# Two layers of cross attention on one core: the product with Wv and the next q taken in turn on TensorE

## The chip, the cores and the metric

The kernel runs on one core of one Trainium2 chip. The metric is the time of the whole program on the device in microseconds (us); lower is better. The kernel before has a median of 1026.28 us over three runs (1025.25 to 1026.63).

## What is computed

There are 32 batch entries, `x` of 224 rows by 512 and a context of 750 rows by 256. Two layers of the same form run one after the other on x; the context is the same for both:

```
q = x Wq + bq ;  k = ctx Wk + bk ;  v = ctx Wv + bv
w = softmax over t of (q k^T / sqrt(512))      # over the 224 rows of x, for each context row
x = layernorm(w v + x) * gamma + beta          # eps 1e-6
```

The softmax runs over the rows of x, so each context row can be normalised by itself. All is in float32.

## The kernel before, in words

**Algebra.** Scores need q k^T only, so the kernel folds `Wq Wk^T` once per layer into a matrix `A` (512 by 256) and multiplies x by it: what it calls q is `x A`, transposed, 256 by 224, held as two halves `l` = 0, 1 of 128 partitions. In the same way w is first multiplied by the raw context (the `o` product, again two halves `l`) and the result by `Wv` (the `pv` product, two halves `h` of 112 rows each). The operands of q, score and pv are split into a rounded high part and a low remainder of type float32r; each product is then high times high, high times low and low times high.

**Units.** A unit is one layer of one batch entry. `a` units are layer 0, `b` units layer 1; a b unit works on the entry whose layer 0 was done three units before. For each unit TensorE makes, in this order: q (two products of 12 matmuls with 224 moving columns and 128 columns of weights), the scores (three pairs of context pieces, 12 matmuls each), o (two products of six float32 matmuls, which the profile records as 12 each), and pv (two products of six matmuls, 512 moving columns, 112 columns of weights). In steady state one pass of the loop body (`turn`) does one a unit and one b unit; each engine has its own `turn`, an order written out by hand, and the engines meet through semaphores only. Each engine takes its instructions in that order, and a wait holds up all that stands behind it on the same engine.

**TensorE's order around the change** (lines 765 to 788). At two places of a pass pv and q products stand next to each other. At the b place the order is pv(b-1,0), q(b,0), pv(b-1,1), q(b,1), and then o(a,0); pv(b-1) belongs to the b unit of the pass before. At the a place it is q(a+1,0), pv(a,0), spread_d(a+1) (two small transposes), pv(a,1), q(a+1,1), and then o(b,0).

**Who takes the results.** ScalarE's `turn` (lines 933 to 967): when a q half is complete (`q_ready`) `q_hi` (L882) rounds it into `qT_hi`; `exps` (L890) makes the exponentials of three context pieces; `normalise` (L906) multiplies three pieces by the inverse sums and raises `probs_done`, after which TensorE may use these pieces in an o product: the first three matmuls of `o_product(u, 0)` need the first three pieces, the other three the second. ScalarE's order around the a place is `q_hi(a+1,0)`, `normalise(b,0)`, `exps(b,1)`, `normalise(b,1)`, `q_hi(a+1,1)`. Around the b place it is `exps(a,0)`, `xT_hi(b,1)`, `xT_hi(a+1,0)`, `exps(a,1)`, `q_hi(b,0)`, `normalise(a,0)`, `normalise(a,1)`, `q_hi(b,1)`. Both layers share the code; the names are as the turn that runs on TensorE has them.

VectorE's `turn` (lines 1271 to 1336) makes the low remainders (`q_lo` L1148, `o_lo` L1187, `xT_lo_part` L1117), adds pv to the residual (`add_pv` L1220), and inverts the exponential sums (`invert_sum` L1181). Around the a place its order has `residual(a,0)`, `residual(a,1)`, `score_max(b,3)`, `invert_sum(b,0)`, `o_lo(a,1)`, two `score_max`, `ctxT_lo`, `add_pv(a,0)`, `q_lo(a+1,0)`, `turn_ctx`, `invert_sum(b,1)`, `half_moments(a,0)`, `add_pv(a,1)` and, some instructions later, `q_lo(a+1,1)`.

**What the products wait for.** `q_product(u, l)` waits until the PSUM bank it shares with o has been read (`oT_lo_done` of the unit two before, and `resid_done` for l = 1), and for the parts of xT. `pv_product(u, h)` waits until its bank was read by the unit before (`y_done`), and for `oT_hi` and `oT_lo`.

Of the kernel before, what the change touches and what calls it, by code (L numbers as in the profile page):

```python
# [14 lines left out]
R_HALF = 1  # L15
# [72 lines left out]
def build_xattn(nc, x, ctx, weights, out):  # L88
    B, T, E = x.shape
    _, M, L = ctx.shape  # L90
    P = 128
    TP, TH = T // 2, 2
    MC = 6
    MP = M // MC
    EC, LC = E // P, L // P
# [9 lines left out]
    with ExitStack() as stack:  # L105
        def sb(name, shape, dt=F32):
            return stack.enter_context(nc.sbuf_tensor(name, shape, dt))

        def bank(name):
            return stack.enter_context(nc.psum_tensor(name, [P, 512], F32))  # L110

        def sem(name):
            return stack.enter_context(nc.semaphore(name))


        A_hi = sb("A_hi", [P, LAYERS, EC, L], F32R)
        A_lo = sb("A_lo", [P, LAYERS, EC, L], F32R)
        Wv_hi = sb("Wv_hi", [P, LAYERS, LC, E], F32R)
        Wv_lo = sb("Wv_lo", [P, LAYERS, LC, E], F32R)
# [29 lines left out]
        xT_hi = sb("xT_hi", [P, 2, EC, T], F32R)  # L149
        xT_lo = sb("xT_lo", [P, 2, EC, T], F32R)  # L150
# [11 lines left out]
        oT_hi = sb("oT_hi", [P, LC, T], F32R)  # L162
        oT_lo = sb("oT_lo", [P, LC, T], F32R)
# [19 lines left out]
        oq_bank = [bank("oq_bank0"), bank("oq_bank1")]  # L183
        pv_bank = [bank("pv_bank0"), bank("pv_bank1")]
# [16 lines left out]
        bq_done = sem("bq_done")  # L201
        A_ready = sem("A_ready")
        A_hi_done = sem("A_hi_done")
        A_lo_done = sem("A_lo_done")
# [5 lines left out]
        Wv_lo_done = sem("Wv_lo_done")  # L210
# [10 lines left out]
        ctxT_lo_done = sem("ctxT_lo_done")  # L221
        xT_ready = sem("xT_ready")
        xT_hi_done = sem("xT_hi_done")
        xT_lo_done = sem("xT_lo_done")
# [3 lines left out]
        q_ready = sem("q_ready")  # L228
# [11 lines left out]
        oT_hi_done = sem("oT_hi_done")  # L240
        oT_lo_done = sem("oT_lo_done")
        resid_done = sem("resid_done")
        pv_ready = sem("pv_ready")
        y_done = sem("y_done")
# [32 lines left out]
        def units(i, j):  # L277

            return (lambda d: Unit(2 * (i + d), j)), (lambda d: Unit(2 * (i + d) + 1, j))
# [14 lines left out]
        PIECES_OF_PAIR = [-(-2 * (p + 1) * MP // PC) for p in range(HALF)]  # L294
# [9 lines left out]
        def is_last(u):  # L304

            return u.j is None and u.u == LAST
# [150 lines left out]
        def _(pe):  # L457
# [110 lines left out]
            def spread_d(u):  # L568

                if not u.real:  # L570
                    return
                pe.wait_ge(dot_done, u.n(m=2))
                b = t_bank[0]
                if u.layer:

                    pe.wait_ge(xT_lo_done, u.n(m=2))
                elif u.past(-1):

                    pe.wait_ge(d_done, u.n(-1))
                else:  # L580

                    pe.wait_ge(ctxT_lo_done, PIECES)
                for h in range(TH):
                    ins = nc.tensor.transpose(b[:, h * TP:(h + 1) * TP], d_col[0:TP, h:h + 1].to_broadcast([TP, P]),
                                              ident[0:TP, 0:TP])
                ins.then_inc(d_ready, 1)

            def q_product(u, l):
                if not u.real:
                    return  # L590
                if u.first and l == 0:
                    pe.wait_ge(A_lo_done, EC * (u.layer + 1))
                if u.first and u.layer == 0:

                    pe.wait_ge(ctxT_lo_done, PIECES_OF_PAIR[l])
                if u.past(-2):

                    pe.wait_ge(oT_lo_done, u.n(-2, 2, l - 1))
                    if l == R_HALF:
                        pe.wait_ge(resid_done, u.n(-2, 2))  # L600
                o = oq_bank[l][:, 0:T]
                for e in range(EC):
                    if l == 0 and e % 2 == 0:
                        pe.wait_ge(xT_hi_done, u.n(m=2, add=e // 2 - 1))
                    nc.tensor.matmul(o, A_hi[:, u.layer, e, l * P:(l + 1) * P], xT_hi[:, u.par, e, :], start=(e == 0), stop=False)  # L605
                    nc.tensor.matmul(o, A_lo[:, u.layer, e, l * P:(l + 1) * P], xT_hi[:, u.par, e, :], start=False, stop=False)  # L606
                for e in range(EC):
                    if l == 0 and e % 2 == 0:
                        pe.wait_ge(xT_lo_done, u.n(m=2, add=e // 2 - 1))
                    ins = nc.tensor.matmul(o, A_hi[:, u.layer, e, l * P:(l + 1) * P], xT_lo[:, u.par, e, :],  # L610
                                           start=False, stop=(e == EC - 1))
                ins.then_inc(q_ready, 1)

            def score_product(u, p):
                if not u.real:
                    return
                if u.layer == 0:
                    pe.wait_ge(ctxT_hi_done, u.batch(PIECES, PIECES_OF_PAIR[p]))
                    pe.wait_ge(ctxT_lo_done, u.batch(PIECES, PIECES_OF_PAIR[p]))
                if u.past(-1) or p == 2:  # L620

                    pe.wait_ge(smax_done, u.n(m=6, add=2 * p - 8))
                b = score_bank[(u.pair0() + p) % 2]
                for c in range(2):
                    cols = slice((2 * p + c) * MP, (2 * p + c + 1) * MP)
                    o = b[0:MP, c * T:(c + 1) * T]
                    for l in range(LC):
                        if p == 0 and c == 0:
                            pe.wait_ge(qT_hi_done, u.n(m=2, add=l - 1))
                        nc.tensor.matmul(o, cT_hi[:, u.slot, l, cols], qT_hi[:, l, :], start=(l == 0), stop=False)  # L630
                        nc.tensor.matmul(o, cT_lo[:, u.slot, l, cols], qT_hi[:, l, :], start=False, stop=False)  # L631
                    for l in range(LC):
                        if p == 0 and c == 0:
                            pe.wait_ge(qT_lo_done, u.n(m=2, add=l - 1))
                        ins = nc.tensor.matmul(o, cT_hi[:, u.slot, l, cols], qT_lo[:, l, :], start=False, stop=(l == LC - 1))  # L635
                ins.then_inc(s_ready, 1)

            def o_product(u, l):
# [22 lines left out]
                                               start=True, stop=True)  # L661
                ins.then_inc(o_ready, 1)

            def pv_product(u, h, at_end=False):
                if not u.real or is_last(u) != at_end:
                    return
                if u.past(-1):

                    pe.wait_ge(y_done, u.n(-1, 2, h - 1))
                if u.first and h == 0:  # L670
                    pe.wait_ge(Wv_lo_done, u.layer + 1)
                if u.first and u.layer == 0:

                    pe.wait_ge(bq_done, h + 1)
                o = pv_bank[h][0:TP, :]
                rows = slice(h * TP, (h + 1) * TP)
                for l in range(LC):
                    if h == 0:
                        pe.wait_ge(oT_hi_done, u.n(m=2, add=l - 1))
                    nc.tensor.matmul(o, oT_hi[:, l, rows], Wv_hi[:, u.layer, l, :], start=(l == 0), stop=False)  # L680
                    nc.tensor.matmul(o, oT_hi[:, l, rows], Wv_lo[:, u.layer, l, :], start=False, stop=False)  # L681
                for l in range(LC):
                    if h == 0:
                        pe.wait_ge(oT_lo_done, u.n(m=2, add=l - 1))
                    ins = nc.tensor.matmul(o, oT_lo[:, l, rows], Wv_hi[:, u.layer, l, :], start=False, stop=(l == LC - 1))
                ins.then_inc(pv_ready, 1)

            def last_o_product(u):

# [75 lines left out]
            def turn(i, j):  # L765
                a, b = units(i, j)
                score_product(a(+0), 0)
                o_product(b(-1), 1)
                transpose_x(b(+0), 0)
                score_product(a(+0), 1)  # L770
                score_product(a(+0), 2)
                transpose_x(b(+0), 1)
                pv_product(b(-1), 0)
                q_product(b(+0), 0)
                pv_product(b(-1), 1)
                q_product(b(+0), 1)
                o_product(a(+0), 0)
                spread_d(b(+0))
                score_product(b(+0), 0)
                score_product(b(+0), 1)  # L780
                o_product(a(+0), 1)
                score_product(b(+0), 2)
                q_product(a(+1), 0)
                pv_product(a(+0), 0)
                spread_d(a(+1))
                pv_product(a(+0), 1)
                q_product(a(+1), 1)
                o_product(b(+0), 0)
            turns(pe, turn, 2)
            last_o_product(last_unit)  # L790
# [813 lines left out]
```

## Time and profile before

| | us |
|---|---|
| median of three runs | 1026.28 |
| time of the profiled execution | 1024.44 |
| its span, first to last instruction | 1022.3 |
| TensorE matmul busy | 992.1 (97%) |
| VectorE busy | 874.6 (86%) |
| ScalarE busy | 664.2 (65%) |
| GpSimd busy | 566.7 (55%) |

The profile is of one execution; the span leaves out 2.1 us around it. Busy time of TensorE counts each matmul from its start to its modelled end, and consecutive matmuls overlap, so 97% says that TensorE hardly ever stood empty, not that it ran at its peak. The cadence has to be read from the starts of consecutive matmuls. A row "x4" of the timeline merges four like instructions; its duration runs from the first start to the last end.

### The profile page before, as it was taken

The numbers are of one execution on the slowest core, as the hardware profiler recorded it, in microseconds if no ns is written. First come the engines' busy times: TensorE is split into PE (matmuls) and PEld (weight loads), VectorE is DVE, ScalarE is ACT, GpSimd is POOL, SyncE is SP. The second block draws the span as 40 slices with busy tenths as digits, with TensorE's granted clock in tenths as the row PEclk, the third lists the DMA queues.
The fourth block names the chain that finished last, engine by engine and source line by source line (L and its number), as shares of the span: only waits on it lengthen the run. The fifth ranks groups of instructions, "written<-read, shape, count | busy, mean of one in ns | idle before, by whom it ended". The sixth has DMA issues, their size and how long they took to land. (4 is left out here: it accounts for less than half of the span.)

```text
span 1022.3 us, 23872 instructions
## 1 busy us (share of the span) xinstructions
PE 992.1 (97%) x6948; PEld 932.4 (91%) x6948; DVE 874.6 (86%) x2609; ACT 664.2 (65%) x1864; POOL 566.7 (55%) x520
## 2 busy tenths in 40 slices
PE   6889999999999999999999999999999999999986
PEld 5789999999999999999999999999999999999975
DVE  3768889898889889888988988898988898888867
ACT  2456667667666767766666776766676677667642
POOL 0114655565665556566555656555565655556574
PEclk9979999999999999999999999999999999999998
DMA  8643345444444544444554443455444345544101
GB/s 229 134 96 74 79 98 115 97 98 101 95 83 100 114 96 96 99 89 87 104 114 96 95 99 82 91 106 110 95 96 100 79 94 110 103 105 98 54 19 37
DMA packets 374246, 98.84 MB, mean 97 GB/s; under 512 B 308520, under 2 KB 357818, under 8 KB 374202
## 3 DMA queue, kind: packets, MB, share of 16 engines
q1 hardware_dynamic: 371370, 96.98, 43.7%
q10 hardware_dynamic: 2832, 1.32, 0.6%
q8 instruction: 22, 0.36, 0.1%
q14 instruction: 22, 0.18, 0.1%
HBM read 83.59 MB, written 14.68 MB: 96 GB/s over the span
## 5 line engine op out<-in xcount | busy, mean ns | idle before, releaser
L654 PE MATMUL oq_bank<-probs,raw 125*128 125x224 f32 x1512 | 307.5, 353 | 3.7 <-ACT probs L906 3.7
L654 PEld LDWEIGHTS oq_bank<-probs,raw 125*128 125x128 f32 x1512 | 276.7, 190 | 4.5 <-issue 3.2
L890 ACT ACTIVATE probs<-probs,neg_max 125x224 f32<-125x224 f32 x378 | 177.8, 472 | 143.5 <-DVE neg_max L1165 143.5
L1477 POOL TENSOR_TENSOR psum<-probs 125x672 f32<-125x672 f32 x63 | 101.6, 1613 | 285.0 <-ACT probs L906 285.0
L630 PE MATMUL score_bank<-qT_hi,cT_hi 128*125 128x224 f32 x768 | 199.8, 287 | 2.8 <-ACT cT_hi L847 1.7
L631 PE MATMUL score_bank<-qT_hi,cT_lo 128*125 128x224 f32 x768 | 189.1, 273 | 0.0
L906 ACT ACTIVATE probs<-probs,rsum 125x224 f32<-125x224 f32 x378 | 150.7, 471 | 10.3 <-DVE rsum L1181 8.9
L1540 POOL TENSOR_TENSOR y_out<-z,gamma_row 112x512 f32<-112x512 f32 x62 | 93.8, 1534 | 114.7 <-ACT z L930 114.7
L630 PEld LDWEIGHTS score_bank<-qT_hi,cT_hi 128*125 128x125 f32 x768 | 145.3, 189 | 7.8 <-issue 5.5
L635 PE MATMUL score_bank<-qT_lo,cT_hi 128*125 128x224 f32 x768 | 147.2, 273 | 0.0
L631 PEld LDWEIGHTS score_bank<-qT_hi,cT_lo 128*125 128x125 f32 x768 | 145.5, 189 | 0.0
L1165 DVE CUSTOM_DVE_ANT_0 probs<-score_bank,d_row 125x224 f32<-125x224 f32 x384 | 139.0, 380 | 6.7 <-PE score_bank L635 3.8
L605 PE MATMUL oq_bank<-xT_hi,A_hi 128*128 128x224 f32 x512 | 121.7, 276 | 0.9 <-DVE w_col L1057 0.6
L606 PE MATMUL oq_bank<-xT_hi,A_lo 128*128 128x224 f32 x512 | 121.5, 275 | 0.0
L1210 DVE SCALAR_TENSOR_TENSOR y<-bv_row,oq_bank,x 112x512 f32<-112x512 f32 x126 | 105.5, 857 | 18.4 <-ACT oT_hi L917 18.3
L635 PEld LDWEIGHTS score_bank<-qT_lo,cT_hi 128*125 128x125 f32 x768 | 115.1, 189 | 0.2 <-DVE qT_lo L1148 0.2
L680 PE MATMUL pv_bank<-Wv_hi,oT_hi 128*112 128x512 f32 x256 | 105.2, 411 | 0.0
L1117 DVE TENSOR_TENSOR xT_lo<-t_bank,xT_hi 128x448 fp32r<-128x448 f32 x128 | 78.8, 616 | 30.2 <-ACT xT_hi L862 30.1
L605 PEld LDWEIGHTS oq_bank<-xT_hi,A_hi 128*128 128x128 f32 x512 | 98.4, 192 | 6.7 <-DVE w_col L1057 0.8
L606 PEld LDWEIGHTS oq_bank<-xT_hi,A_lo 128*128 128x128 f32 x512 | 98.6, 193 | 3.8
L930 ACT ACTIVATE z<-y,nmr,rstd 112x512 f32<-112x512 f32 x126 | 95.5, 806 | 9.7 <-DVE nmr L1252 9.7
L681 PE MATMUL pv_bank<-Wv_lo,oT_hi 128*112 128x512 f32 x256 | 100.6, 393 | 0.0
(122 smaller groups left out, 2024.7 us busy)
## 6 DMA issues: line engine op xcount, KB each, us to landing
raw<-in_ctx_dram SPq DMA_DIRECT2D x64, 375.0 KB
cb<-in_ctx_dram SPq DMA_DIRECT2D x248, 92.0 KB
x<-in_x_dram SPq DMA_DIRECT2D x32, 448.0 KB, 3.6
xb<-in_x_dram SPq DMA_DIRECT2D x124, 112.0 KB, 3.0
out_dram<-y_out SPq DMA_DIRECT2D x31, 448.0 KB, 6.6
cb<-in_ctx_dram SPq DMA_DIRECT2D x124, 3.5 KB
y<-in_L_xattn_Wq_dram SPq DMA_DIRECT2D x2, 512.0 KB, 5.4
Wq_next<-in_L_xattn_Wq_dram SPq DMA_DIRECT2D x2, 512.0 KB, 15.7
```

What stands on the lines that cost most here:

```text
L605: nc.tensor.matmul(o, A_hi[:, u.layer, e, l * P:(l + 1) * P], xT_hi[:, u.par, e, :], start=(e == 0), stop=False)
L606: nc.tensor.matmul(o, A_lo[:, u.layer, e, l * P:(l + 1) * P], xT_hi[:, u.par, e, :], start=False, stop=False)
L630: nc.tensor.matmul(o, cT_hi[:, u.slot, l, cols], qT_hi[:, l, :], start=(l == 0), stop=False)
L631: nc.tensor.matmul(o, cT_lo[:, u.slot, l, cols], qT_hi[:, l, :], start=False, stop=False)
L635: ins = nc.tensor.matmul(o, cT_hi[:, u.slot, l, cols], qT_lo[:, l, :], start=False, stop=(l == LC - 1))
L654: ins = nc.tensor.matmul(o, raw[0:MP, u.slot, c, cols], probs[0:MP, u.par4, c, :], start=(c == 0), stop=(c == MC - 1))
L680: nc.tensor.matmul(o, oT_hi[:, l, rows], Wv_hi[:, u.layer, l, :], start=(l == 0), stop=False)
L890: ins = act.activation(probs[0:MP, u.par4, c, :], probs[0:MP, u.par4, c, :], ACT.Exp, bias=neg_max[0:MP, u.par4, c:c + 1], scale=-1.0, acc ...
L906: ins = act.activation(probs[0:MP, u.par4, c, :], probs[0:MP, u.par4, c, :], ACT.Identity, scale=rsum[0:MP, u.par4, c:c + 1])
L1165: dve.tensor_tensor_reduce(probs[0:MP, u.par4, c, :], b[0:MP, (c % 2) * T:(c % 2 + 1) * T], d_row[0:MP, :], -SCALE, 3.4e38, ALU.add, ALU.m ...
L1210: dve.scalar_tensor_tensor(out=y[0:TP, u.par, h, :], in0=bv_row[0:TP, u.layer, :], scalar=(last_r if at_end else r_psum)[:, h:h + 1], in1= ...
L1477: pool.tensor_tensor(psum3[0:MP, :, :], probs[0:MP, u.par4, 0:HALF, :], probs[0:MP, u.par4, HALF:MC, :], ALU.add).then_inc(psum3_done, 1)
```

## The change

`q_product` and `pv_product` are cut into single matmuls, `q_step` and `pv_step`, with the same waits ahead of the same matmuls. A new function issues one pv matmul and then two q matmuls, six times over. The turn calls it at both places. No matmul, wait or transfer is added or removed; the other engines' programs are untouched. Where one of the two units doesn't exist, or the pv is that of the last unit, the two products are issued whole, pv first. The opening, which is written out by hand, keeps whole products.

```diff
+            Q_STEPS, PV_STEPS = 3 * EC, 3 * LC
+            def q_step(u, l, k):
+                if k == 0:
+                    ... the waits of q_product
+                if k < 2 * EC:
+                    e = k // 2
+                    if l == 0 and k % 4 == 0:
+                        pe.wait_ge(xT_hi_done, u.n(m=2, add=e // 2 - 1))
+                    of = A_lo if k % 2 else A_hi
+                    nc.tensor.matmul(o, of[:, u.layer, e, cols], xT_hi[:, u.par, e, :], start=(k == 0), stop=False)
+                    return
+                e = k - 2 * EC
+                if l == 0 and e % 2 == 0:
+                    pe.wait_ge(xT_lo_done, u.n(m=2, add=e // 2 - 1))
+                ins = nc.tensor.matmul(o, A_hi[:, u.layer, e, cols], xT_lo[:, u.par, e, :], start=False, stop=(e == EC - 1))
+                if e == EC - 1:
+                    ins.then_inc(q_ready, 1)
+            def pv_step(u, h, k):
+                ... in the same way, one of the six matmuls of pv_product
+            def pv_with_q(u, h, v, l):
+                if not (u.real and v.real) or is_last(u):
+                    pv_product(u, h)
+                    q_product(v, l)
+                    return
+                for k in range(PV_STEPS):
+                    pv_step(u, h, k)
+                    q_step(v, l, 2 * k)
+                    q_step(v, l, 2 * k + 1)
 def turn(i, j):
-                pv_product(b(-1), 0)
-                q_product(b(+0), 0)
-                pv_product(b(-1), 1)
-                q_product(b(+0), 1)
+                pv_with_q(b(-1), 0, b(+0), 0)
+                pv_with_q(b(-1), 1, b(+0), 1)
                 ...
                 score_product(b(+0), 2)
-                q_product(a(+1), 0)
-                pv_product(a(+0), 0)
+                pv_with_q(a(+0), 0, a(+1), 0)
                 spread_d(a(+1))
-                pv_product(a(+0), 1)
-                q_product(a(+1), 1)
+                pv_with_q(a(+0), 1, a(+1), 1)
                 o_product(b(+0), 0)
```

## Rows read from the trace of the kernel before

**Rows 1.** The page: busy time by engine; TensorE's granted clock in tenths, 40 slices.

```profile
PE 992.1 (97%) x6948; PEld 932.4 (91%) x6948; DVE 874.6 (86%) x2609; ACT 664.2 (65%) x1864; POOL 566.7 (55%) x520
PEclk9979999999999999999999999999999999999998
```

**Rows 2.** Windows, steady state: stretch, length, busy (count) by engine, clock, DMA.

```profile
110.00:953.00 843.00, 842.47 (x5976) 796.05 (x5975) 747.58 (x2255) 580.66 (x1634) 498.28 (x449) 1.00 0.45 97
```

**Rows 3.** Waits of TensorE, matmuls then weight loads: total us, times, longest.

```profile
PE oq_bank L654 <- ACT probs L906: 3.7, 3, 2.0
...
PEld pv_bank L685 <- DVE oT_lo L1187: 4.7, 13, 1.0
```

**Rows 4.** Timeline of TensorE, the a place: start, us, instruction, count.

```profile
503.04 0.27 PE L605 MATMUL oq_bank<-xT_hi,A_hi 128*128 128x224 f32 x1
...
533.10 0.27 PE L605 MATMUL oq_bank<-xT_hi,A_hi 128*128 128x224 f32 x1
...
533.99 0.61 PE L610 MATMUL oq_bank<-xT_lo,A_hi 128*128 128x224 f32 x4
534.44 0.40 PE L680 MATMUL pv_bank<-Wv_hi,oT_hi 128*112 128x512 f32 x1
...
535.83 0.36 PE L584 MATMUL t_bank<-ident,d_col 112*128 112x112 f32 x2
535.95 0.47 PE L680 MATMUL pv_bank<-Wv_hi,oT_hi 128*112 128x512 f32 x1
...
536.95 0.62 PE L685 MATMUL pv_bank<-Wv_hi,oT_lo 128*112 128x512 f32 x2
537.41 0.27 PE L605 MATMUL oq_bank<-xT_hi,A_hi 128*128 128x224 f32 x1
...
538.74 2.44 PE L654 MATMUL oq_bank<-probs,raw 125*128 125x224 f32 x12
...
562.88 0.27 PE L605 MATMUL oq_bank<-xT_hi,A_hi 128*128 128x224 f32 x1
```

**Rows 5.** Timeline of ScalarE, same place; in brackets the idle time ahead and its releaser.

```profile
534.72 0.45 ACT L882 ACTIVATE qT_hi<-oq_bank,c_col 128x224 fp32r<-128x224 f32 x1 [0.69 <-PE oq_bank L610]
535.07 1.21 ACT L906 ACTIVATE probs<-probs,rsum 125x224 f32<-125x224 f32 x3
536.18 0.47 ACT L890 ACTIVATE probs<-probs,neg_max 125x224 f32<-125x224 f32 x1
...
537.92 1.23 ACT L906 ACTIVATE probs<-probs,rsum 125x224 f32<-125x224 f32 x3 [0.24 <-DVE rsum L1181]
```

**Rows 6.** Timeline near the end: an o product that waited for ScalarE.

```profile
984.32 1.30 PE L654 MATMUL oq_bank<-probs,raw 125*128 125x224 f32 x6
986.46 0.83 PE L654 MATMUL oq_bank<-probs,raw 125*128 125x224 f32 x3 [0.84 <-ACT probs L906]
...
985.18 1.23 ACT L906 ACTIVATE probs<-probs,rsum 125x224 f32<-125x224 f32 x3 [0.24 <-DVE rsum L1181]
```

**Rows 7.** Timelines of TensorE, ScalarE, VectorE at the b place.

```profile
518.51 0.47 PE L680 MATMUL pv_bank<-Wv_hi,oT_hi 128*112 128x512 f32 x1
518.82 0.39 PE L681 MATMUL pv_bank<-Wv_lo,oT_hi 128*112 128x512 f32 x1
...
519.09 0.95 ACT L862 ACTIVATE xT_hi<-t_bank 128x448 fp32r<-128x448 f32 x2
...
521.78 0.69 DVE L1220 TENSOR_TENSOR y<-pv_bank,y 112x512 f32<-112x512 f32 x1
```

**Rows 8.** Timelines of VectorE and TensorE: the other kind of pass, a place.

```profile
505.14 0.35 DVE L1187 TENSOR_TENSOR oT_lo<-oq_bank,oT_hi 128x224 fp32r<-128x224 f32 x1
...
505.31 0.73 PE L685 MATMUL pv_bank<-Wv_hi,oT_lo 128*112 128x512 f32 x2
```

**Rows 9.** Timeline of VectorE after the a place.

```profile
537.71 0.18 DVE L1181 RECIPROCAL rsum<-ssum 125x3 f32<-125x3 f32 x1
...
540.51 0.44 DVE L1148 SCALAR_TENSOR_TENSOR qT_lo<-oq_bank,c_col,qT_hi 128x224 fp32r<-128x224 f32 x1
```

More of the change, by code:

```diff
@@ L586, in spread_d @@
                 ins.then_inc(d_ready, 1)
+            Q_STEPS, PV_STEPS = 3 * EC, 3 * LC
+            def q_step(u, l, k):
+                if k == 0:
+                    if u.first and l == 0:
+                        pe.wait_ge(A_lo_done, EC * (u.layer + 1))
+                    if u.first and u.layer == 0:
+                        pe.wait_ge(ctxT_lo_done, PIECES_OF_PAIR[l])
+                    if u.past(-2):
+                        pe.wait_ge(oT_lo_done, u.n(-2, 2, l - 1))
+                        if l == R_HALF:
+                            pe.wait_ge(resid_done, u.n(-2, 2))
+                o = oq_bank[l][:, 0:T]
+                cols = slice(l * P, (l + 1) * P)
+                if k < 2 * EC:
[11 more added lines that the diff above has]
+                    ins.then_inc(q_ready, 1)
             def q_product(u, l):
@@ L590, in q_product @@
                     return
[L591 to L612, printed above, removed]
+                for k in range(Q_STEPS):
+                    q_step(u, l, k)
             def score_product(u, p):
@@ L662, in o_product @@
                 ins.then_inc(o_ready, 1)
+            def pv_step(u, h, k):
+                if k == 0:
+                    if u.past(-1):
+                        pe.wait_ge(y_done, u.n(-1, 2, h - 1))
+                    if u.first and h == 0:
+                        pe.wait_ge(Wv_lo_done, u.layer + 1)
+                    if u.first and u.layer == 0:
+                        pe.wait_ge(bq_done, h + 1)
+                o = pv_bank[h][0:TP, :]
+                rows = slice(h * TP, (h + 1) * TP)
+                if k < 2 * LC:
+                    l = k // 2
+                    if h == 0 and k % 2 == 0:
+                        pe.wait_ge(oT_hi_done, u.n(m=2, add=l - 1))
+                    of = Wv_lo if k % 2 else Wv_hi
+                    nc.tensor.matmul(o, oT_hi[:, l, rows], of[:, u.layer, l, :], start=(k == 0), stop=False)
+                    return
+                l = k - 2 * LC
+                if h == 0:
+                    pe.wait_ge(oT_lo_done, u.n(m=2, add=l - 1))
+                ins = nc.tensor.matmul(o, oT_lo[:, l, rows], Wv_hi[:, u.layer, l, :], start=False, stop=(l == LC - 1))
+                if l == LC - 1:
+                    ins.then_inc(pv_ready, 1)
             def pv_product(u, h, at_end=False):
@@ L666, in pv_product @@
                     return
[L667 to L686, printed above, removed]
+                for k in range(PV_STEPS):
[4 more added lines that the diff above has]
+                    q_product(v, l)
+                    return
+                for k in range(PV_STEPS):
+                    pv_step(u, h, k)
+                    q_step(v, l, 2 * k)
+                    q_step(v, l, 2 * k + 1)
             def last_o_product(u):
```

## The prediction

> **What bounds the kernel now.** I read the page first. TensorE is busy 97% of the span, the next engine 86%, and the granted clock stands near full speed but in the opening and at the end [rows 1]. The windows give the steady state by itself: in the 843 us from 110 to 953 the matmuls are busy 842.47 us at a clock of 1.00 [rows 2]. So TensorE's own stream is the bound, and anything that makes it stand still shows in full. The list of its waits then says how little it stands now: 3.7 us in three waits for the normalised probabilities, all outside the steady passes, and a weight load that waits for oT_lo in 13 passes [rows 3]. Last I laid the timelines of the three engines side by side at both places of the change, since a kernel that waits this little may still have little to spare.
>
> The passes take 30.06 and 29.78 us in turn (503.04 to 533.10 to 562.88 [rows 4]); the longer kind holds the wait for oT_lo. I price both kinds below.
>
> **Part 1: the pace of TensorE.** The work is the same: per interleaving 6 pv and 12 q matmuls. Before, 12 q take 533.10 to 534.44, 1.34 us or 0.1115 each, and 6 pv take 534.44 to 535.83, 1.39 us or 0.232 each [rows 4]. One pv and two q cost 0.232 + 2 x 0.1115 = 0.455. What interleaving can alter is each matmul's spacing by its neighbour. Both new neighbourhoods stand in the trace. Four steps of 0.1125 lead from the first low matmul of q at 533.99 to the pv at 534.44, the last of them over the load of a 112-column pv weight in place of a 128-column q weight: q isn't quicker with a shorter load behind it. And the two steps from the first low pv at 536.95 over the second to the q at 537.41 take 0.46 against 0.464 [rows 4]: pv before q is as slow as pv before pv, or some 4 ns quicker, below the 10 ns grain of the row. I take that: each interleaving turns five pv-to-pv steps into pv-to-q. The turn runs on TensorE from i = 2; a(i) and a(i+1) both exist up to i = 30, b(i-1) and b(i) up to i = 32, so the a place is interleaved in 29 passes and the b place in 31, two products in each: 120 interleavings, 120 x 5 x 0.004 = 2 us gained. Bounds: the nearest rows of another pace are the o matmuls, where 12 records against 6 take 2.44 against 1.30, so 0.19 for one [rows 4, 6]. Each is of float32 and 224 columns; if it is passed twice that is 448 columns, 0.424 ns a column. At that pace 512 columns take 0.217 and 224 take 0.095, and a triple 0.407: 720 triples x 0.048 = 35 us gained at most. The other bound is 10 ns lost in a triple, 7 us. I stay by the two rows of the very neighbourhoods.
>
> The Trainium skill, "TensorE: Matmul & The Clock Gate", section "LDWEIGHTS (loading the stationary operand)", gives a weight load as its columns divided by 1.2 GHz: 107 ns for 128 columns, 93 for 112. By that the q stream would be paced by its loads (107 against the 0.1115 seen), and a pv matmul would hide one load of each pair, which is what would make the change pay. The row with the 112-column load, 0.1125 where that rule leads one to expect about 0.10, speaks against it; what it would give is the first rival.
>
> **Part 2: what is moved at the a place, and what that does to ScalarE.** Count from the first matmul there as 0 (533.10). Before, q(a+1,0) stands first and its last matmul starts at 11 x 0.1115 = 1.23. ScalarE has been idle for 0.69 us waiting for just this and starts q_hi at 534.72 = 1.62, so 0.39 after it. Behind q_hi in its order stand normalise(b,0), three exponentials, and normalise(b,1), which ends at 537.92 + 1.23 = 539.15: 4.43 us after q_hi began, with no gap but 0.24 for the inverted sums [rows 5]. The o product after the place starts at 538.74 = 5.64, and its seventh record, the first to need the second three pieces, at 5.64 + 6 x 0.19 = 6.78; the pieces are there at 6.05. Room: 0.73.
>
> After, q(a+1,0) shares TensorE with pv(a,0). Its last matmul is the last of six triples: 5 x 0.455 + 0.232 + 0.11 = 2.62, that is 1.39 later. ScalarE was waiting for it, so all behind moves with it: q_hi at 3.01, normalise(b,1) ends at 3.01 + 4.43 = 7.44. TensorE gets to the seventh record at 6.79 as before (the same matmuls are issued by then). How soon it runs after the release: near the end of this trace an o product did wait; ScalarE ended at 985.18 + 1.23 = 986.41 and the matmul started at 986.46, 0.05 later, but the three records took 0.83 where two steps of 0.19 and a normal 0.35 make 0.73, so some 0.10 more [rows 6]. The record thus counts as starting at 7.59: a stall of **0.80 us**, in each of 29 passes: **+23.2 us**. Bounds: 0.70 without the 0.10; 0.88 if the load is paid again. Nothing hides it: TensorE's next instructions stand behind the waiting one, and the q and pv results it owes to others come no earlier.
>
> In the longer kind of pass there is more. There o_lo(a,1) ends at 505.14 + 0.35 = 505.49, 2.45 after the place's start, and the last pv matmul of h = 0, which needs it, waits already [rows 8]. After, that matmul is due at 5 x 0.455 = 2.27 instead of 2.50 and runs at 2.45 + 0.15 = 2.60: 0.33 lost, ahead of the last q matmuls, and so on top of the 0.80. Such passes cost 0.28 extra before. If they are as many as the 13 waits [rows 3], +0.7 us. Whether they will be is open: none, -3.6; all 29, 29 x 0.33 - 3.6 = +6.
>
> What else is needed earlier there has room: q(a+1,1) starts 1.2 us sooner, and wants residual(a,1), which stands before o_lo(a,1) in VectorE's order and so is done by 2.45. pv(a,0) comes to start first instead of second; its oT_hi is older than the residual that was made from the same o.
>
> **Part 3: the b place.** Here pv stood first already, so the last matmul of q(b,0) keeps its time and ScalarE's chain there too; pv(b-1,0) gets ready 1.2 us later, at about 2.4 + 0.45 after 518.51, that is 521.4, and VectorE only takes it at 521.78 [rows 7]. But q's fifth matmul, the first to need xT_hi(b,1), comes forward from 1.4 + 4 x 0.11 to: first step 0.31 (518.51 to 518.82), then q q, pv, q q, pv: 0.22 + 0.23 + 0.22 + 0.23, in all 1.21. xT_hi(b,1) is the first of two that start at 519.09 and take 0.95 together, so it ends between 519.57 and 519.64, 1.06 to 1.13 [rows 7]. With 0.05 to 0.15 for the release the matmul runs at 1.11 to 1.28: a stall of 0 to 0.07, I take 0.03, 31 x 0.03 = +1 us, bounds 0 and 0.1 (3 us).
>
> **Sum.** 23.2 + 0.7 + 1 - 2 = +23 us on the profiled execution's 1024.44, whose span is 1022.3: 1047.4. That execution stands 1.84 below the median, and so the forecast for the median is 1047.4 + 1.8 = **1049 us**.
>
> What is late next: VectorE, in its order, reaches invert_sum(b,1) at 537.71 = 4.61, when the exponentials have just ended [rows 9]; after, they end 1.39 later and VectorE stands. add_pv(a,1), the moments and q_lo(a+1,1), which began at 540.51 = 7.41 [rows 9], follow some 1.2 us later, and would end at about 9.0. The score product that needs it follows the o product, at 5.64 + 12 x 0.19 + 0.80 = 8.72, and comes to it with its sixth matmul, some 0.5 us on: 9.2. It just passes.
>
> **Rivals.** (1) The loads are what paces q, and a load under a 512-column matmul is free. For: 0.1115 against the 0.095 of a streaming-bound 224 columns. Against: the step of 0.1125 over a 112-column load. Price: 0.0165 for one q of each triple, 0.1 an interleaving; at the b place 62 x 0.1 = 6.2 gained; at the a place only the shortening of the chain ahead of the stall counts, 29 x 0.1 = 2.9, as the second interleaving there only brings TensorE to the wait sooner. In place of my 2: 1049 - 7 = 1042.
>
> (2) The delay doesn't die out at VectorE: q_lo(a+1,1), or the layer norm's chain behind it, comes 0.2 us and more late for the score product or for the transposes of z. For: the margin above is only 0.2. Against: VectorE is idle for 14% of the span, some 4 us a pass, in which it can catch up [rows 1]. Price 0.2 to 0.6 a pass, with 0.4 x 29 = 12: 1061.
>
> (3) Not slower: every matmul runs at the pace of the o rows, 0.407 a triple. Then the b place gains 4 x 0.14 = 0.57 a pass, and at the a place the last q matmul is at 5 x 0.407 + 0.217 + 0.095 = 2.35, the seventh record at 2.35 + 0.39 + 4.43 + 0.15 = 7.32 against 6.78: 0.54 lost. The two cancel: 31 x 0.57 - 29 x 0.54 = 2 gained, 1024. The change pays only from there on; at any slower triple the a place wins. For it: only that another kind of matmul keeps that pace. Against it: all steps in rows 4.
>
> **How the numbers follow.** Forecast 0.67; (1) 0.12; (2) 0.16; (3) 0.05. The forecast's own range, with the bounds of its terms, is 1043 to 1057; to hold 8 in 10 with part of (1) and (2) on either side it is 1041 to 1061. A measurement of this kernel tells 0.2% (2 us) from no change. Faster by more than that needs (3) and a bit of luck: 0.03; within it 0.02; slower 0.95.
>
> **What would show it.** Right: a wait of TensorE L654 for ScalarE L906 in about 29 passes, some 0.7 to 0.8 us each, which becomes the first in its list of waits; ScalarE's idle time before L882 up by 1.2 to 1.4 a pass; VectorE waiting for L890 at L1181; passes of 30.5 to 30.9 us; triples of 0.45. Wrong: triples of 0.44 or less (rival 1 or 3); the o product after the a place without a wait, which would mean that ScalarE's chain wasn't tied to q(a+1,0); or a new wait at the score product (rival 2).

## The result and the profile after

The changed kernel takes 1062.66 us, the median of four runs (1061.49 to 1063.48), against 1025.76 us for the kernel before beside it. The ratio is 1.036 (95% interval 1.034 to 1.038): 37 us slower. The forecast was 1049, with a range of 1041 to 1061: the right sign and the first of the two waits, but 14 us too little, and the result lies outside the range.

The page after, its head and its busy times, answers to [rows 1]: TensorE has fallen from 97% to 95%, at the same clock.

```profile
span 1061.0 us, 23872 instructions
...
PE 1006.1 (95%) x6948; PEld 938.9 (88%) x6948; DVE 878.4 (83%) x2609; ACT 663.4 (63%) x1864; POOL 566.9 (53%) x520
...
PEclk9979999999999999999999999999999999999998
```

The window of [rows 2] again, now of the changed kernel: 818 of 843 us busy where it was 842.

```profile
110.00:953.00 843.00, 818.07 (x5730) 766.05 (x5729) 721.01 (x2163) 555.70 (x1566) 479.70 (x433) 1.00 0.44 94
```

The waits after, of matmuls and of weight loads (total, times, longest), answer to [rows 3]. The wait for the normalised probabilities, seen 3 times before, is there in nearly every pass, as forecast. The second row was not in the forecast: the score product waits for `cT_lo`. Rival (2) had a wait at the score product, but for another instruction. The view puts the idle time between two matmuls at less than their starts show, since it counts the modelled drain of the last one as busy.

```profile
PE oq_bank L666 <- ACT probs L935: 20.0, 32, 2.0
PE score_bank L642 <- DVE cT_lo L1138: 7.6, 22, 0.4
...
PEld oq_bank L666 <- ACT probs L935: 27.6, 30, 1.2
PEld score_bank L642 <- issue: 19.7, 31, 1.9
PEld pv_bank L700 <- DVE oT_lo L1216: 4.2, 12, 0.7
```

Now one pass of the changed kernel at the a place, TensorE first. It answers to [rows 4]; read the starts.

```profile
552.61 0.40 PE L695 MATMUL pv_bank<-Wv_hi,oT_hi 128*112 128x512 f32 x1
552.85 0.27 PE L611 MATMUL oq_bank<-xT_hi,A_hi 128*128 128x224 f32 x1
...
555.09 0.38 PE L616 MATMUL oq_bank<-xT_lo,A_hi 128*128 128x224 f32 x2
...
558.17 1.30 PE L666 MATMUL oq_bank<-probs,raw 125*128 125x224 f32 x6
560.06 1.40 PE L666 MATMUL oq_bank<-probs,raw 125*128 125x224 f32 x6 [0.58 <-ACT probs L935]
561.80 0.34 PE L642 MATMUL score_bank<-qT_hi,cT_hi 128*125 128x224 f32 x1 [0.34 <-DVE cT_lo L1138]
```

The seventh record of the o product is due at 558.17 + 6 x 0.19 = 559.31 and starts at 560.06: 0.75 late, and its own step is 0.10 longer than another's (1.40 against 1.30 for six). The last q matmul is the second of the row at 555.09. The score product, where it waits for nothing, starts 2.12 after the o product (in the kernel with everything moved, below: 539.36 to 541.48). Here it is due at 558.17 + 2.12 + 0.85 = 561.14 and starts at 561.80: 0.66 late.

ScalarE and VectorE in the same stretch, the first answering to [rows 5], the second to [rows 9]:

```profile
555.58 0.45 ACT L911 ACTIVATE qT_hi<-oq_bank,c_col 128x224 fp32r<-128x224 f32 x1 [2.03 <-PE oq_bank L616]
555.92 1.22 ACT L935 ACTIVATE probs<-probs,rsum 125x224 f32<-125x224 f32 x3
...
558.78 1.23 ACT L935 ACTIVATE probs<-probs,rsum 125x224 f32<-125x224 f32 x3 [0.24 <-DVE rsum L1210]
```

```profile
558.57 0.18 DVE L1210 RECIPROCAL rsum<-ssum 125x3 f32<-125x3 f32 x1 [1.56 <-ACT probs L919]
558.66 0.67 DVE L1255 BATCH_NORM_STATS2 bn<-y 112x6 f32<-112x512 f32 x1
559.24 0.67 DVE L1249 TENSOR_TENSOR y<-pv_bank,y 112x512 f32<-112x512 f32 x1
559.95 0.69 DVE L1255 BATCH_NORM_STATS2 bn<-y 112x6 f32<-112x512 f32 x1
560.56 0.42 DVE L1263 BATCH_NORM_AGGREGATE mv<-bn 112x2 f32<-112x6 f32 x2
560.90 0.56 DVE L1138 TENSOR_TENSOR cT_lo<-t_bank,cT_hi 128x384 fp32r<-128x384 f32 x1
```

This is the whole path. ScalarE stands 2.03 us (0.69 before) for the last q matmul, VectorE stands 1.56 us in `invert_sum(b,1)` for ScalarE's exponentials, and behind five more instructions comes `ctxT_lo(a+1,1)`. It ends at 561.46, and the score product starts 0.34 after that. Here are the same two rows of the kernel before, in the pass of [rows 4]:

```profile
540.04 0.56 DVE L1109 TENSOR_TENSOR cT_lo<-t_bank,cT_hi 128x384 fp32r<-128x384 f32 x1
...
540.94 0.35 PE L630 MATMUL score_bank<-qT_hi,cT_hi 128*125 128x224 f32 x1
```

It ended at 540.60, and the score product started 0.34 after it too, where it was due at 538.74 + 2.12 = 540.86. So it waited already, for 0.08, too little for the list of waits to show, and that cost nothing: the first step of the score product is 0.19 behind the wait (540.94 to 541.13) and 0.27 without one (541.48 to 541.75 in the kernel with everything moved), so that its second matmul starts 2.39 after the o product in both. Where I saw a room of 0.73 at the o product, this path had none; the change added 0.58 there.

The passes: in the kernel before the a place starts at 143.36 and, 27 passes on, at 951.49, a mean of 29.93 us; in the changed kernel the same two, with 27 passes between them, are

```profile
146.33 0.39 PE L695 MATMUL pv_bank<-Wv_hi,oT_hi 128*112 128x512 f32 x1
...
988.87 0.40 PE L695 MATMUL pv_bank<-Wv_hi,oT_hi 128*112 128x512 f32 x1
```

a mean of 31.20. The difference, 1.27 us, times 29 passes is 37 us: all of the loss lies in the steady passes. Means of passes below are made this way, over the same 27. Two kinds of pass take turns, as before: the one shown above, now of 31.10 us (29.78 before), and a longer one, now mostly of 31.47 (30.06 before).

### The profile page after: what moved, and what is told of

The parts are those of the page before. It is cut to its first block and busy times, and to the rows that moved or that the text cites. A ratio compares the mean times of both kernels' runs of the same rounds, so it can differ in the third digit from the quotient of the medians.

```text
span 1061.0 us, 23872 instructions
## 1 busy us (share of the span) xinstructions
PE 1006.1 (95%) x6948; PEld 938.9 (88%) x6948; DVE 878.4 (83%) x2609; ACT 663.4 (63%) x1864; POOL 566.9 (53%) x520
## 5 line engine op out<-in xcount | busy, mean ns | idle before, releaser
L666 PE MATMUL oq_bank<-probs,raw 125*128 125x224 f32 x1512 | 316.8, 356 | 20.0 <-ACT probs L935 20.0
L611 PE MATMUL oq_bank<-xT_hi,A_lo 128*128 128x224 f32 x512 | 140.2, 276 | 0.0
L611 PE MATMUL oq_bank<-xT_hi,A_hi 128*128 128x224 f32 x512 | 139.1, 273 | 1.0 <-DVE w_col L1086 0.6
L616 PEld LDWEIGHTS oq_bank<-xT_lo,A_hi 128*128 128x128 f32 x512 | 95.4, 191 | 10.2
L911 ACT ACTIVATE qT_hi<-oq_bank,c_col 128x224 fp32r<-128x224 f32 x128 | 56.7, 443 | 76.3 <-PE oq_bank L616 75.5
L700 PE MATMUL pv_bank<-Wv_hi,oT_lo 128*112 128x512 f32 x256 | 100.5, 397 | 1.8 <-DVE oT_lo L1216 0.6
```

The lines of the kernel that those rows point to most:

```text
L611: nc.tensor.matmul(o, of[:, u.layer, e, cols], xT_hi[:, u.par, e, :], start=(k == 0), stop=False)
L666: ins = nc.tensor.matmul(o, raw[0:MP, u.slot, c, cols], probs[0:MP, u.par4, c, :], start=(c == 0), stop=(c == MC - 1))
```

## The experiments

Theory C says that the loss is the lateness of q(a+1,0), carried over ScalarE and VectorE. Its rivals are that interleaving costs TensorE by itself (I) and that the later pv holds up VectorE (V). Four kernels undo or isolate parts of the change.

**First pair of the a place whole.**

```diff
-                pv_with_q(a(+0), 0, a(+1), 0)
+                q_product(a(+1), 0)
+                pv_product(a(+0), 0)
```

> As the changed kernel, but at the a place the first pair stands as before: q(a+1,0) whole, then pv(a,0) whole. The other three pairs stay interleaved. Theory C (the loss is that q(a+1,0) is complete 1.34 us later and ScalarE's chain behind it with it): both waits of TensorE vanish, and what is left is the pace of the interleaved triples, 0.444 against 0.455 in the changed kernel's trace: 31 x 2 + 29 = 91 interleavings x 0.066 = 6 us gained, about 1020 us. Rival I (turning between two accumulations costs TensorE by itself): three of four interleavings stay, so about three quarters of the loss, 1054 us. Rival V (pv becomes ready 1.2 us later and VectorE falls behind): three of the four late pv products stay, so 1045 us or more.

Measured: 1031.18 us, ratio 1.0043 (1.0026 to 1.0061). One pair of the four undone takes back 31 of the 37 us, which neither rival allows. But it isn't the 1020 of theory C: the passes take 30.09. TensorE's o product doesn't wait any more (its 12 records run through), but the score product still comes 0.47 late (545.22, where 542.63 + 2.12 = 544.75; 0.08 before), and VectorE shows why:

```profile
541.64 0.18 DVE L1211 RECIPROCAL rsum<-ssum 125x3 f32<-125x3 f32 x1
541.74 0.66 DVE L1256 BATCH_NORM_STATS2 bn<-y 112x6 f32<-112x512 f32 x1
542.61 0.69 DVE L1250 TENSOR_TENSOR y<-pv_bank,y 112x512 f32<-112x512 f32 x1 [0.21 <-PE pv_bank L700]
543.34 0.69 DVE L1256 BATCH_NORM_STATS2 bn<-y 112x6 f32<-112x512 f32 x1
543.95 0.42 DVE L1264 BATCH_NORM_AGGREGATE mv<-bn 112x2 f32<-112x6 f32 x2
544.29 0.56 DVE L1139 TENSOR_TENSOR cT_lo<-t_bank,cT_hi 128x384 fp32r<-128x384 f32 x1
```

`invert_sum(b,1)` is on time, but `add_pv(a,1)` now waits for pv(a,1), which the interleaving of the second pair completes later, and `ctxT_lo` stands behind it. So rival V is right for a small part: a second source feeds the same wait.

**The b place alone interleaved.** The a place as in the kernel before.

> Interleaved at the b place only; the a place as in the kernel before. Theory C: 62 interleavings x 0.066 = 4 us gained and no wait, about 1022 us. Rival I: half of the loss, 1044 us. Rival V: about half, 1044 us. It also prices the wait for xT_hi(b,1), which I put at 0.03 us a pass: were it 0.2, the gain would be gone and the time 1025 us or more.

Measured: 1024.54 us, ratio 0.999 (0.9978 to 1.0001), in passes of 29.87 against 29.93. At the b place there is nothing to lose and next to nothing to gain; that excludes I. The 4 us expected were too many (see the pace, below).

**Only the first pair of the a place interleaved.**

> Only the first pair of the a place, pv(a,0) with q(a+1,0), is interleaved; the three others stand as before. Theory C: this pair alone carries the whole loss, with 29 interleavings of gain in place of 120: 1062.7 + 91 x 0.066 = about 1069 us at most, 1065 to 1069 (part of the gain was swallowed by the waits anyhow). Rivals I and V: a quarter of the loss, 1035 us.

Measured: 1063.15 us, ratio 1.0376 (1.0356 to 1.0395), passes of 31.24. The one pair carries all of it. The time is 2 us below what I expected: the other three pairs had less gain to lose than I had counted.

**Nothing interleaved, only the order of two products changed.**

```diff
-                q_product(a(+1), 0)
-                pv_product(a(+0), 0)
+                pv_product(a(+0), 0)
+                q_product(a(+1), 0)
```

> Nothing is interleaved. At the a place the first two products change places: pv(a,0) whole, then q(a+1,0) whole; the rest as before. The last matmul of q(a+1,0) starts at 1.39 + 1.23 = 2.62 after the place's start, as late as when interleaved. Theory C: the whole loss without any gain: 29 passes x (0.80 + 0.6) on 1026, so 1066 to 1071 us, with the same two waits. Rivals that need the interleaving itself: 1026 us.

Measured: 1081.75 us, ratio 1.0551 (1.0522 to 1.0579), passes of 31.95. That is the loss without any interleaving, and more than forecast. Its waits (TensorE's matmuls) say what the rest is:

```profile
PE oq_bank L666 <- ACT probs L939: 18.7, 32, 2.0
PE pv_bank L700 <- DVE oT_lo L1220: 16.3, 16, 1.5
PE score_bank L642 <- DVE cT_lo L1142: 7.5, 22, 0.4
```

The same two waits stand there, and a third, 1 us in 16 passes: pv whole and first asks for `oT_lo` before VectorE has it, and q behind it comes later still. The interleaved form hides part of that, so interleaving as such is not the culprit but a mitigation of the order.

**A smaller dose.** Only the first pair of the a place, four q matmuls to one pv.

```diff
+def pv_with_q(u, h, v, l, n=2):
                 for k in range(PV_STEPS):
                     pv_step(u, h, k)
-                    q_step(v, l, 2 * k)
-                    q_step(v, l, 2 * k + 1)
+                    for m in range(n * k, min(n * k + n, Q_STEPS)):
+                        q_step(v, l, m)
```

> As the kernel in which only the first pair of the a place is interleaved, but with four q matmuls to one pv matmul, so that q(a+1,0) is complete after three pv matmuls: its last matmul starts at 3 x 0.23 + 11 x 0.11 = 1.9 instead of 2.57. Theory C, in proportion: normalise(b,1) ends 0.66 earlier, at 6.73, against the 6.68 at which TensorE comes for it, so the wait at the o product shrinks from 0.74 to about 0.1 to 0.2 and the one at the score product to nearly nothing: 1026 + 29 x 0.15 = about 1030 us. If interleaving as such costs, it stays above 1040. On the pace: if a q matmul is quicker only when its weights and the next ones were loaded under a pv matmul, the first step after pv is 0.103 and the others 0.111.

Measured: 1039.71 us, ratio 1.0125 (1.0099 to 1.0151), passes of 30.38. The o product's wait has shrunk to 0.12 in one kind of pass and to nothing in the other, as forecast. The time isn't 1030, because the score product's wait has not shrunk at all, 0.66 as in the changed kernel (545.43 + 2.12 + the 0.12 by which the o product is still slowed = 547.67):

```profile
539.82 0.40 PE L695 MATMUL pv_bank<-Wv_hi,oT_hi 128*112 128x512 f32 x1
...
545.43 2.56 PE L666 MATMUL oq_bank<-probs,raw 125*128 125x224 f32 x12
548.33 0.34 PE L642 MATMUL score_bank<-qT_hi,cT_hi 128*125 128x224 f32 x1 [0.34 <-DVE cT_lo L1141]
```

This run settles how the two waits are related. Count the score product's start from the start of the place, in like passes: 540.94 - 533.10 = 7.84 before; 548.33 - 539.82 = 8.51 here; 561.80 - 552.61 = 9.19 in the changed kernel. Those are 0, 0.67 and 1.35 late; the last q matmul is late by 0, 0.66 and 1.34. One to one, from zero: in this kind of pass the path to the score product had no room, and every delay of q(a+1,0) comes out of it in full. In the longer kind VectorE is late already in the kernel before, by its own `residual(a,1)` (last section); there the score product starts at 8.10, 8.51 and 9.54 and the last q matmul at 1.23, 1.89 and 2.93, so that 0.66 of delay costs 0.41 and 1.70 costs 1.44: the path had a room of 0.25. The wait at the o product only takes part of that delay earlier, and adds nothing of its own as long as it is the smaller.

**The second wait's cause moved.** The changed kernel with three lines moved.

```diff
 scalar:
+                ctxT_hi(a(+0), 1)
                 q_hi(a(+0), 1)
-                ctxT_hi(a(+0), 1)
 vector:
                 add_pv(a(-1), 1)
+                ctxT_lo(a(+0), 1)
+                q_lo(a(+0), 1)
                 half_moments(a(-1), 1)
                 moments(a(-1), 0)
                 moments(a(-1), 1)
-                ctxT_lo(a(+0), 1)
-                q_lo(a(+0), 1)
```

> The changed kernel with the second wait's cause moved: ScalarE makes ctxT_hi(a+1,1) ahead of q_hi(a+1,1) (both behind normalise(b,1)), and VectorE makes ctxT_lo(a+1,1) and q_lo(a+1,1) ahead of half_moments(a,1) and the moments. The chain up to normalise(b,1) is untouched. If the missing 14 us are the score product's wait for ctxT_lo, behind a VectorE that invert_sum(b,1) held up: the wait at the o product stays at 0.74 a pass, the one at the score product goes, 29 x 0.5 = 14 less: 1048 us. If VectorE's lateness as such is what costs (it comes out later in the pass), it stays near 1062.

Measured: 1050.15 us, ratio 1.0236 (1.0217 to 1.0255), passes of 30.82.

```profile
552.34 1.30 PE L666 MATMUL oq_bank<-probs,raw 125*128 125x224 f32 x6
554.22 1.40 PE L666 MATMUL oq_bank<-probs,raw 125*128 125x224 f32 x6 [0.58 <-ACT probs L935]
555.48 0.34 PE L642 MATMUL score_bank<-qT_hi,cT_hi 128*125 128x224 f32 x1
```

The o product waits as in the changed kernel, the score product starts 1.26 after its seventh record instead of 1.74, so its 0.66 have shrunk to 0.18. That is 12.5 us less in the time, of the 14 that my forecast missed, and the time is the forecast's within 1.2 us.

**The first wait's cause moved.**

```diff
 scalar:
-                q_hi(a(+0), 0)
                 normalise(b(-1), 0)
                 exps(b(-1), 1)
+                q_hi(a(+0), 0)
```

> The changed kernel with one line moved on ScalarE: q_hi(a+1,0) stands behind exps(b,1) instead of ahead of normalise(b,0), so that what doesn't need q no longer waits for it. TensorE's program is that of the changed kernel. Theory C: normalise(b,0) and the exponentials end at about 3.5 after the place's start, q_hi at 3.9, VectorE's q_lo, turn_ctx and invert_sum(b,1) follow by 4.9, normalise(b,1) ends at about 6.2, before the 6.7 at which TensorE needs it: no wait at either product, and all 120 interleavings gain: 1026 - 8 = 1018 us, faster than both kernels. Rivals I and V: TensorE's order and the times of pv are unchanged, so about 1062 us.

Measured: 1043.66 us, ratio 1.017 (1.0153 to 1.0187), passes of 30.58. Half of the loss goes, with TensorE's program untouched, but it isn't 1018. The delay went the other way round the same loop: `q_lo(a+1,0)` on VectorE now waits for the later `q_hi`, and `turn_ctx` and `invert_sum(b,1)` stand behind it, so ScalarE gets the inverted sums late, here by 1.07:

```profile
548.46 0.43 ACT L911 ACTIVATE qT_hi<-oq_bank,c_col 128x224 fp32r<-128x224 f32 x1
549.96 1.23 ACT L935 ACTIVATE probs<-probs,rsum 125x224 f32<-125x224 f32 x3 [1.07 <-DVE rsum L1210]
```

In this pass, which starts at 544.89, that does no harm at the o product: `normalise(b,1)` ends at 551.19, 6.30 after the start, and the seventh record is due at 6.69. Only the score product is late, by 0.44. In the longer kind of pass `q_hi` comes 4.74 after the start instead of 3.57, since `normalise(b,0)` stood 1.27 for `invert_sum(b,0)`, behind VectorE's longer `residual(a,1)`. There `normalise(b,1)` ends at 7.47, and the seventh record is 0.47 late:

```profile
582.43 1.40 PE L666 MATMUL oq_bank<-probs,raw 125*128 125x224 f32 x6 [0.30 <-ACT probs L935]
```

So the passes take 30.02 and 31.19 us in turn: most of what is left of the loss lies in the longer ones.

**All of it moved.** ScalarE as in the two kernels above; on VectorE:

```diff
                 add_pv(a(-1), 0)
+                invert_sum(b(-1), 1)
                 q_lo(a(+0), 0)
                 turn_ctx(a(+0), 1)
-                invert_sum(b(-1), 1)
                 half_moments(a(-1), 0)
+                ctxT_lo(a(+0), 1)
                 add_pv(a(-1), 1)
+                q_lo(a(+0), 1)
                 half_moments(a(-1), 1)
                 moments(a(-1), 0)
                 moments(a(-1), 1)
-                ctxT_lo(a(+0), 1)
-                q_lo(a(+0), 1)
```

> The changed kernel with the chain cut at every place found so far. ScalarE: q_hi(a+1,0) behind exps(b,1), ctxT_hi(a+1,1) ahead of q_hi(a+1,1). VectorE: invert_sum(b,1) ahead of q_lo(a+1,0), ctxT_lo(a+1,1) ahead of add_pv(a,1), q_lo(a+1,1) ahead of half_moments(a,1). TensorE's program is the changed kernel's. Theory C (the whole loss is the path from q(a+1,0), and from pv(a,1), over ScalarE and VectorE to the o product and the score product): no wait at either product; what remains is the quicker q step behind each pv, 5 x 0.008 = 0.04 an interleaving, 4.8 us in all, less the oT_lo wait, 0.36 in half of the passes against 0.11 before, some 3 to 4 us: 1022 to 1027 us. If TensorE's interleaving costs something of its own that the waits hid, it stays above 1030.

Measured: 1025.04 us, ratio 1.0001 (0.9986 to 1.0015), passes of 29.93. With TensorE issuing exactly what it issues in the changed kernel, the 37 us are gone, by moving five calls on two other engines. The product rows stand close, without a wait:

```profile
539.36 2.44 PE L666 MATMUL oq_bank<-probs,raw 125*128 125x224 f32 x12
541.48 0.43 PE L642 MATMUL score_bank<-qT_hi,cT_hi 128*125 128x224 f32 x1
```

**The same moves on the kernel before, without interleaving.**

> The kernel before (nothing interleaved) with the same moves on ScalarE and VectorE as the changed kernel with everything moved. It tells how much of that kernel's time is the moves and how much the interleaving. The path had no room before, and stood at the score product for 0.1 to 0.2 us in about 12 passes: 2 us gained, 1024 us; the interleaved one should then stand within 3 us of it, on either side.

Measured: 1025.54 us, ratio 1.0007 (0.9993 to 1.0021). The moves by themselves bring nothing that can be measured, nor does interleaving on top of them. The 2 us expected don't come: in the short passes the score product now starts without its wait of 0.08, which cost nothing (above), and in the longer ones it starts 0.17 sooner, and TensorE then stands as much longer in front of the transposes of z.

**The second pair's share.** The first kernel of this section with the VectorE order above (but `invert_sum` in its old place) and `ctxT_hi` first on ScalarE.

> The kernel with the first pair of the a place whole (1031 us), with ctxT_hi(a+1,1) ahead of q_hi(a+1,1) on ScalarE, and on VectorE ctxT_lo(a+1,1) ahead of add_pv(a,1) and q_lo(a+1,1) ahead of half_moments(a,1). There the score product still stood 0.3 to 0.4 us a pass though q(a+1,0) was on time. Theory C2: VectorE waited in add_pv(a,1) for a pv(a,1) that interleaving made 1.2 us late, and ctxT_lo stood behind it. Then the wait goes and the passes take 29.7: 1031 - 29 x 0.33 = about 1021 to 1023 us. If it was ScalarE or the transposes that were late, nothing changes: 1031.

Measured: 1026.76 us, ratio 1.0015 (1.0002 to 1.0027), from 1.0043: the score product's wait is gone, which fits pv(a,1) as its source there but doesn't single it out, since `ctxT_lo` now also stands ahead of other instructions. What shows the source is the rows of the first kernel above: `add_pv(a,1)` starts 5.57 after the place's start, 5.28 in the kernel before, and `ctxT_lo` 7.25, 6.94 before. But the passes take 29.99, not 29.7, and the next wait opens at the transposes of z. I put that down to the moments, now behind, which make z late; no run isolates it:

```profile
PEld t_bank L564 <- ACT z L960: 2.7, 13, 0.7
PEld t_bank L564 <- issue: 2.3, 11, 0.2
```

No kernel here beats the one before by more than can be measured.

## Why the prediction was right and wrong

**The bound** (TensorE's stream, with all waits in full): right; the loss is the sum of its waits.

**The wait at the o product**: right. Forecast: last q matmul 2.62 after the place's start, `q_hi` at 3.01, seventh record effectively 0.80 late. Measured from 552.61: last q matmul about 2.57, `q_hi` 2.97, 0.75 late plus 0.10 in its own step. The kernel in which only this wait is left in full stands at 1050.15 against my 1049; that it comes so near is in part luck, since three small terms were off and cancel (below).

**"What is late next ... It just passes"**: this is the step that failed. I followed VectorE's lateness to `q_lo(a+1,1)`, which the score product needs in its sixth matmul, and not to `ctxT_lo(a+1,1)`, which stands ahead of it in the same order and which the score product needs in its first. The room was none where I had computed 0.2 for `q_lo`, and even that was too much: I let the o product take 12 x 0.19 = 2.28 until the score product starts, where the trace has 2.12, and VectorE came 1.35 later, not 1.2. I also took the release to cost 0.05 to 0.15, as at the o product and at `xT_hi`. Here it is 0.34 between the end of `ctxT_lo` and the first matmul, in both kernels, in the passes that run in the hardware loop (`Fori` in the program; 22 in the changed kernel, 0.34 or 0.35 in each). In the seven passes of the changed kernel outside it the same matmul behind the same four semaphore waits (`ctxT_hi_done`, `ctxT_lo_done`, `smax_done`, `qT_hi_done`) starts 0.10 to 0.11 after the end of `ctxT_lo`:

```profile
935.58 0.52 DVE L1138 TENSOR_TENSOR cT_lo<-t_bank,cT_hi 128x384 fp32r<-128x384 f32 x1
...
936.21 0.34 PE L642 MATMUL score_bank<-qT_hi,cT_hi 128*125 128x224 f32 x1
```

What differs in the program is that the values waited for are constants there, and inside the loop are worked out from its register. In the trace TensorE's queue then has register operations among these waits, of which those of L634, the wait for `smax_done`, are

```profile
L634 PEldq ALU_OP  x110: 32/32/32, 221.2 to 892.9; - x110
```

and at 561.50 to 561.75 a wait, such an operation and another wait stand between the end of `ctxT_lo` and the weight load. That they are what turns 0.10 into 0.34 is a reading of the trace; no run isolates it. Price of the whole wait: 0.58 in the pass above and 0.43 in the longer kind (of the 1.27 us a pass 0.85 are the o product's); the kernel without this wait measures it directly, 12.5 us, nearly the whole miss.

It was in my rivals: (2) named this mechanism at 0.2 to 0.6 a pass and 1061 us, with a chance of 0.16, by the wrong instruction, and its sign, a new wait at the score product, is what the list of waits shows; against it I set VectorE's idle time as an average over the pass, which says nothing about one path through it.

**The pace of TensorE**: near, by a different step than the one I took. I had pv before q 4 ns quicker than pv before pv. In the changed kernel the pv steps are unchanged (0.23), and it is the q step right behind a pv that is shorter. Here are rows of the b place after, answering to the first rows of [rows 7]:

```profile
600.63 0.47 PE L695 MATMUL pv_bank<-Wv_hi,oT_hi 128*112 128x512 f32 x1
...
601.83 0.33 PE L611 MATMUL oq_bank<-xT_hi,A_hi 128*128 128x224 f32 x1
601.99 0.27 PE L611 MATMUL oq_bank<-xT_hi,A_lo 128*128 128x224 f32 x1
602.10 0.39 PE L695 MATMUL pv_bank<-Wv_lo,oT_hi 128*112 128x512 f32 x1
```

The grain of 10 ns hides it in one triple; added up over the places with no wait in them, the first q step is 0.103 where the others are 0.111, and a triple 0.447. Five of the six triples gain it over the order before, 0.04 an interleaving, 4.8 us over 120 (I said 2). My later 0.066, in the expectations above, counted it against the wrong reference. At the b place most of it is spent again on `xT_hi(b,1)`, for which the fifth q step (601.83 to 601.99) is 0.16 instead of 0.10 (I said a wait of 0.03): from its first pv matmul to the o product the place takes 5.484 on the mean, 5.502 before, so that 0.02 of 0.08 are left. The rule of the Trainium skill ("TensorE: Matmul & The Clock Gate", section "LDWEIGHTS (loading the stationary operand)") gives the 112-column load 14 ns less than the 128-column one, by which I estimate about 0.10 for the q matmul ahead of it; that one still takes 0.11 (601.99 to 602.10), so the trace doesn't follow it there.

**The wait for oT_lo**: its size was right, its price was not. The longer kind of pass, 12 weight loads in the list of waits, loses 0.36 by it now (5.92 against 5.56). I set against that the 0.28 by which such a pass was longer before, as if all of it were this wait. The starts give the wait 0.11 (5.75 from the place's start to the o product, 5.64 in the short kind); 0.15 more lie between the o product and the score product (2.35 there, 2.20 in the short kind), and are the wait for `cT_lo` that I overlooked. So the 0.28 held the missing path, and the term is 12 x 0.25 = 3 us instead of 0.7. It is also why the kernel with everything moved ends level: its passes take 29.67 and 30.12 us in turn, but for two of 30.66 and 30.81, mean 29.93.

**The sum**: 24.7 us at the o product (29 x 0.85) and 12.5 at the score product make 37.2; the pace's 4.8 us gained are about spent on oT_lo (3) and xT_hi (31 times 0.06, about 2), as the kernel with everything moved shows by standing level with the one before. Measured: 36.9. The first term is that of the loop's passes; the seven outside it lose 0.77 there, not 0.85.

## What to carry to other kernels

When a producer is moved, follow its delay through every queue to each consumer on the bounding engine, and take each one's first need, not the nearest or the best known: the tightest may be an unrelated instruction that only stands behind the delayed one in another engine's order (here a context piece behind the inverse of a softmax sum). An engine's average idle time is no margin for a path. And where orders are written out by hand, a reordering that costs the bounding engine nothing can still be paid in full through the others, until their orders are moved with it. What a release costs belongs to the place, too: here one wait was over in 0.05, and four whose values come out of a loop register in 0.34.

## What was not expected of the hardware

A matmul of 224 columns that follows one of 512 takes 0.103 to the next start instead of 0.111, although 128 columns of weights are loaded behind it as behind most others; the second one takes 0.111 although only 112 columns are loaded behind it. So neither the columns nor the load alone give the step; no run here settles what does.

The passes come in two kinds, and one VectorE instruction goes with them. In the long kind `residual(a,1)` starts just behind GpSimd's multiplication and takes 1.83 us instead of 0.75:

```profile
583.66 1.83 DVE L1239 SCALAR_TENSOR_TENSOR y<-bv_row,oq_bank,x 112x512 f32<-112x512 f32 x1
...
583.64 2.99 POOL L1569 TENSOR_TENSOR y_out<-z,gamma_row 112x512 f32<-112x512 f32 x2 [3.59 <-ACT z L959]
```

In the steady passes of both kernels, before and changed, GpSimd's starts 0.01 to 0.02 ahead 11 times each, and each time the residual takes 1.82 or 1.83; where the residual starts first, by as little as 0.07, it takes 0.75 or 0.76. It looks as if the one holds up the other when it starts first; no run moved either.
